# A graph network on one core: the second half of the pass over all nodes moves into the gather of h

## The reference

```python
h = relu(layernorm(x));  x = x + L0(h)     # L0: layernorm with gamma, beta; Chebyshev (3 weights); attention, 4 heads
h = relu(layernorm(x));  x = x + L1(h)     # L1: without messages this is layernorm(h) * gamma + beta
```

## Time and profile before

| | |
|---|---|
| three runs, median (lowest to highest) | 6076.15 us (6075.95 to 6082.46) |
| profiled execution, span | 6087.0 us |
| busy: PE, DVE, ACT, POOL | 66%, 70%, 40%, 61% |
| granted TensorE clock, mean | 0.763 |

### The profile page before, as it was taken

One profiled execution on the slowest core, in us unless ns is written; L12 is line 12 of the kernel. 1 busy time (PEld: TensorE's weight loads), 2 busy tenths in 40 slices (PEclk: granted clock), 3 DMA queues, 4 the chain that ended last, 5 costly groups with the idle time before them and its releaser, 6 DMA issues. The chain is left out here.

```text
span 6087.0 us, 72236 instructions
## 1 busy us (share of the span) xinstructions
PE 4038.1 (66%) x15366; PEld 1893.8 (31%) x15414; DVE 4283.8 (70%) x6878; ACT 2416.3 (40%) x5349; POOL 3717.3 (61%) x3646
## 2 busy tenths in 40 slices
PE   8996777777577779976762887688855545653110
PEld 4443444454333323321111444233322212221000
DVE  8776999999777745540006999799955558997442
ACT  0002767677433312222222776333322226774221
POOL 7773005555577767757771443766547767774777
PEclk9998999999888855556665888888866657886555
DMA  5433555555444422223332333333334433332221
GB/s 72 62 50 62 124 129 165 158 166 160 121 106 106 102 54 63 62 67 89 93 93 61 113 115 100 73 82 83 78 93 131 130 104 71 74 77 63 66 73 52
DMA packets 531259, 569.33 MB, mean 94 GB/s; under 512 B 296530, under 2 KB 311000, under 8 KB 529545
## 3 DMA queue, kind: packets, MB, share of 16 engines
q1 hardware_dynamic: 310522, 434.91, 24.4%
q0 software_dynamic: 116816, 104.86, 8.8%
q10 hardware_dynamic: 103840, 28.71, 3.7%
HBM read 328.73 MB, written 303.31 MB: 104 GB/s over the span
## 5 line engine op out<-in xcount | busy, mean ns | idle before, releaser
L1034 POOL DMA_INDIRECT l_got<-d_x,l_near x1176 | 1161.6, 988 | 575.6 <-issue 435.8
L1042 POOL DMA_INDIRECT ln_xd<-d_xt,idsE x392 | 393.7, 1004 | 654.0 <-PE ps L348 368.5
L729 PE MATMUL ps<-hot_lo,hot_w 128*128 128x512 bf16 x2304 | 507.0, 380 | 15.5 <-DVE hot_lo L674 13.0
L2274 POOL DMA_INDIRECT out<-fi_res,fi_near x392 | 381.8, 974 | 182.3 <-issue 118.6
L1034 POOL DMA_INDIRECT p_got<-d_sums,p_near x392 | 399.3, 1019 | 149.7 <-issue 116.6
L1034 POOL DMA_INDIRECT p_got<-d_h,p_near x392 | 377.6, 963 | 160.7 <-issue 116.2
L615 POOL DMA_INDIRECT d_pos<-place,near x392 | 395.8, 1010 | 124.9 <-issue 118.3
L1034 POOL DMA_INDIRECT p_got<-d_ext,p_near x392 | 382.7, 976 | 138.9 <-issue 118.4
L1706 POOL TENSOR_TENSOR at_own<-at_hd,at_al 128x1024 f32<-128x1024 f32 x49 | 191.8, 3914 | 368.2 <-ACT at_al L1800 218.2
L1465 DVE SCALAR_TENSOR_TENSOR et_hid<-et_hid 128x512 f32<-128x512 f32 x49 | 34.0, 694 | 460.3 <-ACT et_hid L1489 460.3
L322 PE MATMUL ps<-ident,fi_sums 64*128 64x64 f32 x392 | 53.2, 314 | 425.7 <-DVE fi_sums L1208 425.7
(11 more groups left out here) (375 smaller groups left out, 10952.5 us busy)
## 6 DMA issues: line engine op xcount, KB each, us to landing
d_x<-ln_x SPq DMA_DIRECT2D x196, 256.0 KB, 2.3
l_xd<-d_x SPq DMA_DIRECT2D x147, 256.0 KB, 2.9
d_ext<-ln_ext SPq DMA_DIRECT2D x98, 264.0 KB, 2.4
d_xt<-in_x_wide ACTq DMA_DIRECT2D x49, 520.0 KB
ln_x<-in_x SPq DMA_DIRECT2D x98, 256.0 KB
d_h<-ln_hb SPq DMA_DIRECT2D x98, 256.0 KB
d_x<-l_x SPq DMA_DIRECT2D x98, 256.0 KB
out<-d_x SPq DMA_DIRECT2D x49, 512.0 KB
```

The source lines that it names most:

```text
L729: last = nc.tensor.matmul(bank(h), hot_w[:, r, k], hot_lo[:, r, 512 * h:512 * h + 512], start=False, stop=False)
L1034: nc.gpsimd.indirect_dma_start(out=out[:, q], out_offset=None, in_=source, in_offset=bass.IndirectOffsetOnAxis(ap=ids[:, q:q + 1], axis=0) ...
L1042: nc.gpsimd.indirect_dma_start(out=out[:, q], out_offset=None, in_=source, in_offset=bass.IndirectOffsetOnAxis(ap=ids[:, g, q:q + 1], axis=0),
L2274: nc.gpsimd.indirect_dma_start(out=out, out_offset=bass.IndirectOffsetOnAxis(ap=near[:, r, q:q + 1], axis=0), in_=res[:, r, q], in_offset= ...
```

## The change

`NormLagged` replaces `NormTwice` in the node pass: the variance of both norms is formed from the same three sums in three small operations, and the square root gives one gain, not two. Its parts lie in other steps of the loop. The loop of `lone_nodes` ends with x1; it has four lags, rings of 8 for x and the gathered rows. The whole second half (norm, `cm1`, x2) moves to `attention_sources`, where one turn of 49 takes 2048 nodes (tiles of 128 x 1024, loaded from and stored to DRAM by SP). The order of all engines there is written anew; the scores of both halves are made by one product of 128 x 512. The beta row is added as a bf16 product of 65 rows, of which three hold the parts of a split fp32 value (`ones_split`, `beta_split`, prepared in `degrees` by `split_rows`, 20 small operations for the two rows); `gat_b` is added the same way, and the linear part of the second leaky function is a product with `gmean_slope`, so ACT makes one part where it made two. The positions are held as fp32, so ACT writes the factor and the position into `ext` in one operation.

The degree column is written by 16 DMAs of 6272 pieces, all issued by ACT at the stage's start. POOL's gathers wait for these and for a free slot of 8, not for turns. SP stores the gathered groups, one per 1.6 turns from its turn 20. `gather_kept` has no bounds check. `rows_by` is also used in `gated_messages` and changes there too.

```diff
 FIRST_TILES = 96
-COLUMN_PARTS = 32
-FIRST_GATHER = COLUMN_PARTS - 4
-GATHER_TURNS = NODE_GROUPS - FIRST_GATHER - 2
+COLUMN_PARTS = 16
+WIDE = 2 * S
+NODE_RING = 8
+EXT_LATE, H_LATE, X1_LATE = 5, 7, 7
+XD_LATE = 20
+XD_TURNS = NODE_GROUPS - XD_LATE
...
+    def scale(self, nc, dve, g, r, ticks):
+        first = r % 2
+        s0, s1, s2 = (self.sums[:, k] for k in ((1, 0, 2), (0, 2, 1))[first])
+        yield ticks[0]
+        dve.wait_ge(self.squared, g + 1)
+        nc.vector.reduce_sum(self.sums, self.four[:, first:first + 3], AX_X).then_inc(self.step, 1)
+        yield ticks[1]
+        dve.wait_ge(self.step, g * 4 + 1)
+        nc.vector.scalar_tensor_tensor(out=self.a, in0=s1, scalar=1.0 / C, in1=s1, op0=ALU.mult, op1=ALU.mult
+                                       ).then_inc(self.step, 1)
+        nc.vector.scalar_tensor_tensor(out=self.b, in0=s0, scalar=EPS, in1=s2, op0=ALU.mult, op1=ALU.add
+                                       ).then_inc(self.step, 1)
+        yield ticks[2]
+        dve.wait_ge(self.step, g * 4 + 3)
+        nc.vector.tensor_tensor(self.b, self.b, self.a, ALU.subtract).then_inc(self.varied, 1)
+        yield ticks[3]
+        dve.wait_ge(self.rooted, g + 1)
+        nc.vector.reciprocal(self.gain, self.sd).then_inc(self.step, 1)
...
+    def square(self, nc, act, g, r, tick):
+        yield tick
+        act.wait_ge(self.centred, g + 1)
+        nc.scalar.activation(self.y(r), self.xc, ACT.Relu).then_inc(self.relu, 1)
+    def square_rest(self, nc, act, g, r, tick):
+        yield tick
+        act.wait_ge(self.relu, g + 1)
+        nc.scalar.activation(self.xc, self.xc, ACT.Square)
+        nc.scalar.activation(self.y2, self.y(r), ACT.Square).then_inc(self.squared, 1)
+    def root(self, nc, act, g, tick, floor):
+        yield tick
+        act.wait_ge(self.varied, g + 1)
+        nc.scalar.activation(self.sd, self.b, ACT.Sqrt, scale=1.0 / C, bias=floor).then_inc(self.rooted, 1)
...
-def rows_by(nc, out, paired, weights, beta, W):
-    nc.tensor.matmul(out, W.ones_row[:], beta.rearrange("a s c -> a (s c)"), start=True, stop=False)
+def rows_by(nc, out, paired, weights, W):
+    nc.tensor.matmul(out, W.ones_split[:], W.beta_split[:], start=True, stop=False)
...
             def _(pool):
                 hold(pool, m["columns"], 16 * COLUMN_PARTS)
-                for e in range(GROUPS + 1):
-                    if e < GROUPS:
-                        hold(pool, m["x2_done"], FIRST_GATHER + e * GATHER_TURNS // GROUPS)
-                        hold(pool, xd_st[e % RING], 16 * (e // RING))
-                        gather_kept(nc, D.xt, dstE, e, xd[:, e % RING], got_x[e % RING], NP_ - 1)
-                    if e > 0:
-                        r = (e - 1) % RING
-                        hold(pool, got_x[r], 128 * ((e - 1) // RING) + 128)
-                        nc.gpsimd.dma_start(group_rows(D.xd)[e - 1], xd[:, r]).then_inc(xd_st[r], 16)
-                for r in range(RING):
-                    pool.wait_ge(xd_st[r], 16 * of_slot(r, GROUPS))
+                def gather(i, r, e):
+                    hold(pool, xd_st[r], i * 16)
+                    gather_kept(nc, D.xt, dstE, e, xd[:, r], got_x[r])
+                for e in range(GROUPS):
+                    gather(e // NODE_RING, e % NODE_RING, e)
...
+                def load(g):
+                    r = g % NODE_RING
+                    after(sp, m["x1_done"], g - NODE_RING + 1)
+                    sp.dma_start(x[:, r], group_rows(A["x"])[g]).then_inc(x_in[r], 16)
+                    after(sp, m["tabbed"], g - RING + 1)
+                    sp.dma_start(tail[:, g % RING, 0], by_group(D.dinv)[g]).then_inc(tab_in[g % RING], 16)
+                    sp.dma_start(tail[:, g % RING, 1], by_group(D.pos)[g]).then_inc(tab_in[g % RING], 16)
+                def store_ext(g):
+                    sp.wait_ge(m["tabbed"], g + 1)
+                    sp.dma_start(by_group(D.ext)[g], ext[:, g % RING].rearrange("p s c -> p (s c)")
+                                 ).then_inc(ext_st[g % RING], 16)
+                def store_h(g):
+                    sp.wait_ge(m["hb_done"], g + 1)
+                    sp.dma_start(group_rows(D.h_lone)[g], hb[:, g % RING]).then_inc(h_st[g % RING], 16)
+                def store_x1(g):
+                    sp.wait_ge(m["x1_done"], g + 1)
+                    sp.dma_start(group_rows(D.x1_lone)[g], x1[:, g % RING]).then_inc(stored[g % RING], 16)
+                def store_xd(e):
+                    r = e % NODE_RING
+                    sp.wait_ge(got_x[r], 128 * (e // NODE_RING) + 128)
+                    sp.dma_start(group_rows(D.xd)[e], xd[:, r]).then_inc(xd_st[r], 16)
+                edge = 0
+                for s in range(NODE_GROUPS + X1_LATE + 1):
+                    for late, part in ((0, load), (EXT_LATE, store_ext), (H_LATE, store_h), (X1_LATE, store_x1)):
+                        if 0 <= s - late < NODE_GROUPS:
+                            part(s - late)
+                    while edge < GROUPS and s >= XD_LATE + edge * XD_TURNS // GROUPS:
+                        store_xd(edge)
+                        edge += 1
...
+                def begin(i, r, g):
+                    dve.wait_ge(x_in[r], i * 16 + 16)
+                    yield from norm.centre(nc, dve, g, x[:, r], (0, 3))
+                def scale(i, r, g):
+                    yield from norm.scale(nc, dve, g, r, (1, 2, 4, 7, 8))
+                    nc.vector.tensor_tensor(norm.y(r), norm.y(r), norm.spread(norm.gain), ALU.mult
+                                            ).then_inc(m["ya_done"], 1)
...
+                ring_loop(dve, NODE_GROUPS, [begin], [scale], [h], [first_sum], ring=NODE_RING)
...
+                    nc.tensor.matmul(bank(1), W.ones_split[:], W.gat_b_split[:], start=True, stop=False)
+                    for q in range(S // 2):
+                        at = slice(P * q, P * q + P)
+                        nc.tensor.matmul(bank(1)[:, at], hf[:, r % 2, at], W.gmean_slope[:], start=False, stop=False)
+                        last = nc.tensor.matmul(bank(1)[:, at], rest[:, at], W.ident[:], start=False, stop=q == S // 2 - 1)
+                    last.then_inc(m["u_rows"], 1)
+                ring_loop(pe, NODE_GROUPS, [], [], [base, mean], [rows], ring=NODE_RING)
...
-                def columns(i, r, g):
-                    if isinstance(g, int) and g < COLUMN_PARTS:
-                        act.dma_start(column[g], factors[:, g].unsqueeze(2), allow_slow_non_contiguous=True
-                                      ).then_inc(m["columns"], 16)
...
+                for k in range(COLUMN_PARTS):
+                    act.dma_start(column[k], factors[:, k].unsqueeze(2), allow_slow_non_contiguous=True
+                                  ).then_inc(m["columns"], 16)
...
+                    nc.scalar.activation(rest[:], bank(3), ACT.Relu, scale=0.99, bias=col["gat_b_rest"]
+                                         ).then_inc(m["u_done"], 1)
...
-def gather_kept(nc, source, ids, g, out, landed, limit):
+def gather_kept(nc, source, ids, g, out, landed):
     for q in range(S):
         nc.gpsimd.indirect_dma_start(
             out=out[:, q], out_offset=None, in_=source,
-            in_offset=bass.IndirectOffsetOnAxis(ap=ids[:, g, q:q + 1], axis=0),
-            bounds_check=limit, oob_is_err=False).then_inc(landed, 16)
+            in_offset=bass.IndirectOffsetOnAxis(ap=ids[:, g, q:q + 1], axis=0)).then_inc(landed, 16)
...
+        x1 = t("lb_x1", [P, RING, WIDE, C])
+        ybf, x2 = t("lb_ybf", [P, 2 * HALF]), t("lb_x2", [P, 2, WIDE, C])
...
                 def load(i, r, g):
+                    after(sp, m["x2_done"], g - RING + 1)
+                    sp.dma_start(x1[:, r], wide_rows(D.x1_lone)[g]).then_inc(x1_in[r], 16)
+                    after(sp, m["got_t"], g - RING + 1)
+                    sp.wait_ge(hs_st[r], i * 16 + 16)
+                    sp.dma_start(near[:, r], D.ls[g]).then_inc(inn[r], 16)
+                    after(sp, m["et_mm1"], g - 1)
+                    sp.dma_start(ea[:, r % 2], pairs(A["ea_pairs"])[g]).then_inc(ea_in[r % 2], 16)
...
+                def store_nodes(i, r, g):
+                    sp.wait_ge(m["x2_done"], g + 1)
+                    sp.dma_start(wide_rows(D.x2_lone)[g], x2[:, r % 2]).then_inc(x2_st[r % 2], 16)
+                ring_loop(sp, GROUPS, [load], [], [], [store_rows, store_factors], [store_scores, store_nodes])
...
+                def transposed(i, r, g):
+                    yield 0
+                    hold(pe, m["yb_done"], g + 1)
+                    hold(pe, m["ybf_done"], g)
+                    transpose_pairs(nc, bank(4, 2), norm.y(r), W, WIDE).then_inc(m["yb_t"], 1)
+                    yield 2
+                    hold(pe, m["ybf_done"], g + 1)
+                    hold(pe, m["x2_done"], g)
+                    for h in (0, 1):
+                        last = rows_by(nc, bank(6 + h), ybf[:, HALF * h:HALF * h + HALF], W.cm1, W)
```

(8 more changed lines are left out.)

385 lines of the change are left out of this document (206 added, 179 removed).

## The result

The changed kernel takes **5939.7 us** (median of 4 runs, 5931.1 to 5948.5) against 6079.3 for the kernel before beside it: ratio 0.977, 95% interval 0.976 to 0.978. It is faster by 140 us; 337 were predicted. The profiled execution spans 5942.4 us against 6087.0.

A forecast was written before the change was run, and what follows sets the result against it. The node pass was taken as bound by DVE, the gather of h by POOL. Terms of -353 (node pass), +15 (gather of h) and +1 (small edits) sum to -337 us, from 6076.15 to 5739 us; range 5650 to 5850.

The forecast's parts named there:

- The column, 70 us of the sum: Start of the node pass: sixteen column DMAs hold ACT, so no relu runs for 70 us.
- rival 1: Column in the node pass: ACT is not held, node turns start at 557, 5676 us in all; chance 0.20.
- upper bound of 137: Column in the node pass: the longest time allowed for its 100,352 pieces, 65 to 137 us, 75 taken.
- The node turn, 98 x 6.4: Node pass: 98 turns of 6.4 us, set by the chain between DVE, ACT and PE, 627 us.
- the 4% added on top: Node pass: mean turn taken 4% longer than the clean one, as before the change, 6.4 us for 6.2.
- Rival 2: Node pass: one more 512-wide product exposed each turn, 7.5 us a turn, 108 more, 5847 us; chance 0.14.
- The gather of h, +15: Gather of h: the added node work hides almost wholly under POOL's 10.0 us a turn; cost 15 us, bounds 0 and +88.
- for clock dips: Gather of h: a turn taken at 10.3 us instead of POOL's 10.0 to allow for falls of PE's clock.
- Rival 3: Gather of h: PE keeps a low clock, DVE turn 11.8 us, 88 us instead of 15, 5812 us; chance 0.10.
- Rival 4: Gather of h: nothing overlaps between turns, 20.9 us each, 534 us more there, 6258 us in all; chance 0.02.
- POOL beside a busy VectorE, 21 us at worst: Gather of h: indirect DMAs slow from 0.963 to 1.017 us beside busy DVE, 21 us at worst, within the range.
- Small edits, +1: Degree stage, fold stage, later residual and gathers without bounds check: together 1 us more, the bf16 row product counted as 0.

## Why the prediction was wrong

The direction was right, the size was not: -140 against -337, outside the range. By the stretches of the profiled executions the miss is 88 in the node pass plus 122 in the gather of h, less 18 elsewhere. The step that failed is the chain of the gather of h; the column is a term that was mis-sized.

- **The column, 70 us of the sum.** That an issue behind a DMA of thousands of pieces holds its engine was right, and rival 1 fell. Mis-sized was the rate: 1550 pieces per us came from a DMA that lay in the fast start; of the two rows, the 733 beside large copies was near the truth, and I had taken the value nearest to the wrong end. Measured 146.5, 76.5 of the 88 us. My upper bound of 137 was nearly enough, but the forecast's own figure wasn't. The Trainium skill (DMA: Bandwidth & Descriptors, Issuing engines are not separate DMA queues) calls the time to initiate a DMA "usually small relative to the DMA itself"; these sixteen held their engine 146.5 us, and from the first issue to the last landing they took 159.
- **The node turn, 98 x 6.4.** Measured 6.58 in the mean (694.77 to 1333.0 over 97 turns), 18 us more in all, of which 5 come back because the lags took 13 us and not 18. The chain named was the right one; the hand-overs to TensorE, 0.3 us each, were left out, so the clean turn is 6.6 and not 6.2, and the 4% added on top hid half of that by luck. This is read from the timeline and was not tested by a run. Rival 2's exposed product did not come. POOL's gather ended before the nodes, at 1245 against the 1250 forecast, but that agreement is luck: it began at 708.6 and not at 625, and waited only 50.7 us for free slots.
- **The gather of h, +15.** This step failed; measured 137. I added up each engine's work, found all under POOL's 10.0 us, and followed the chain only from the product to x2. I did not go on along ScalarE's queue, where the root stands behind copies that wait for TensorE. The 10.3 us that I took "for clock dips" is what this loop makes with TensorE at its high level; that held in 13 of 48 turns, and 35 took 12.5 to 14.3. Rival 3 had 11.8 us a turn from the low clock and was the nearest, but it took the low clock as given and the chain as closed at x2, where the turn read takes 13.2. The runs show that the 12.7 us need both, the root's place and the low clock: with the root first the turn is 10.6 us, with the pauses filled 11.3, and in both POOL is the bound. Rival 4, all in series, stayed far.
- **POOL beside a busy VectorE, 21 us at worst.** In the kernel after the gathers did grow, from 0.963 to 1.044 us, 32 us in all, hidden under the late p_near. With the chain mended they became the bound. The Trainium skill (SBUF — State Buffer, Who interferes with whom) says that a VectorE instruction with two inputs in SBUF contends with a GpSimd instruction that reads SBUF. Centre and product are of that kind, and the runs agree: 1.7 us for a gather that begins beside them, 0.94 once one input lies in PSUM.
- **Small edits, +1.** The stages ahead of the node pass end within 1.3 us of where they did. The shorter row product in `gated_messages` was put at 0; that stage is 6.6 us shorter, and no run tells whether the product is the reason.

## What to carry to other kernels

Sums of busy time don't show a loop's turn. Follow the chain around the whole turn, through every queue it passes: an instruction that is ready early but stands in order behind one that waits for a late engine is part of the chain. When work is moved under a bound engine, ask what the pauses do to TensorE's granted clock and what the new neighbour does to the gathers. When two remedies differ, look first at what bounds the loop behind each of them. And take a rate for a long transfer from a row that lasts as long.

## What the runs showed of the hardware

- Four-byte writes to DRAM: a fast start of about 3000 pieces in 2 us, then 663 to 666 per us from ScalarE (600 to 620 us, with 32 DMAs and with 16; the hold is the same, 144.4 and 146.5 us), 490 from POOL, 556 with both. With both, the other transfers are slowed (90 GB/s in all instead of 175, from 620 to 680 us).
- An indirect DMA on POOL of 128 rows takes 0.94 us, and up to 2.0 if it begins while VectorE is in an instruction with two large SBUF operands, broadcast or not: what that one had left and 0.82 us. If VectorE's instruction begins later, it stays at 0.94; a triple reduction or an operand in PSUM leaves it there too.
- Twelve useless transposes a turn on TensorE raised its granted clock from 0.76 to 0.92 in the stage and shortened the kernel by 1.3%.
